# Splitting the second layer's projections into three bf16 parts: the subtractions on TensorE inside the PSUM bank, all casts on ScalarE

## The chip, the cores and the metric

The kernel runs on one core of a Trainium2 chip. A core has five engines, each with its own in-order queue of instructions: TensorE (PE, matmuls), VectorE (DVE), ScalarE (ACT), GpSimd (POOL) and SyncE (SP, which here only issues DMAs). They work on SBUF and on PSUM, whose banks take the matmuls' sums, and they wait for one another through semaphores. The metric is the device time of one execution, in microseconds (us).

## The reference

Four blocks work on x of 4 x 512 tokens x 256, each with a layer norm before it and a residual around it: attention with rotary embedding ("a"), a mixture of experts ("f"), differential attention ("b"), and the mixture of experts again ("h"). The change touches the third:

```python
q = (query @ Wq.T).reshape(B, T, 2 * H, D).transpose(0, 2, 1, 3)   # H = 16, D = 8: 32 heads of 8
k = (query @ Wk.T).reshape(B, S, 2 * H, D).transpose(0, 2, 1, 3)
v = (query @ Wv.T).reshape(B, S, H, 2 * D).transpose(0, 2, 1, 3)
attn = jnp.einsum('bhtd,bhsd->bhts', q * scaling, k)
attn = jax.nn.softmax(attn + causal, axis=-1)
attn = attn.reshape(B, H, 2, T, S)
attn = attn[:, :, 0] - lam * attn[:, :, 1]     # lam = exp(sum(lq1 * lk1)) - exp(sum(lq2 * lk2)) + const
```

## The kernel before

Scores are computed with bf16 operands and yet near fp32's precision: each value of q and k is written as the sum of three bf16 parts, high, middle and low (high is the cast of the value, middle the cast of what is left, low the cast of what is then left). The 8 numbers of a head times 6 products of parts fill 48 rows of a matmul.

**The prologue of layer "b"** makes these parts. It goes over B = 4 batches of 512 tokens, each in eight pieces k = 0 to 7, and every engine has its own function that lists its share of the pieces in a fixed order: `pe_piece`, `dve_piece_b`, `act_proj_b`, `pool_attn`, `sp_attn`. For one batch:

- k = 0 to 2: TensorE turns the normed tiles (`pe_turn`, L1295), ScalarE copies them out (`act_tile_T`, L612).
- k = 1 to 3: TensorE computes v (`pe_v`, L1315) in the two banks `pair_ps[:, 0, 0]` and `pair_ps[:, 0, 1]`, ScalarE copies it out (`act_v`, L621 and L622).
- k = 4 to 7: TensorE computes one block of q or k for each piece (`pe_block`, L1354, four fp32 matmul instructions of 512 columns on the same two banks, block i in bank i % 2). Blocks 0 and 2 are q, 1 and 3 are k.
- Split of a block: ScalarE casts the bank to `parts[:, i, 0]` (`act_block`, L641); VectorE subtracts it from the bank into SBUF, `px[:, i]` (`dve_rest`, L836), which frees the bank (`b_rest`); GpSimd casts `px` to `parts[:, i, 1]` and subtracts once more into `parts[:, i, 2]` (`pool_parts`, L492 and L493), which signals `b_lo`.
- SyncE stores the parts of a block to DRAM when `b_lo` comes (`sp_store_parts`, L339 and L342), and once batch 0 is stored begins to load them back as stacks of 48 rows (`sp_stacks`, L319 and L328).
- VectorE also adds up the residual of the next batch (`dve_back`, L1059) and norms it (L813).

**The first score units** are spread over the same pieces. To find the row maxima for the softmax, TensorE computes scores (`pe_first_scores`, L1451 to L1475) and VectorE reduces each pair of banks with a maximum (`dve_first_max`, L956). There are 30 units before the attention proper: 6 in batch 1 (two each after pieces 5, 6 and 7), 12 in batch 2, 12 in batch 3, by `spread = (0, 2, 3, 5, 6, 8, 9, 10, 12)` over the pieces. They alternate between two pairs of banks, so unit i waits until the maximum of unit i - 2 is taken.

**The end of the prologue**: after its last cast ScalarE computes two exponentials for lam (L691), for which it loads a table; VectorE, in piece 7 of the last batch, waits for them (`dve_lambda`, L891) before it takes the maxima of units 28 and 29. Then slots begin: TensorE's first unit of transposed scores (L1426) goes into the pair of banks that the projections used, and so waits for `b_rest` of all 16 blocks; the next score unit waits for the maximum of unit 28. In the slots ScalarE takes exponentials (L706), GpSimd masks (L519), TensorE multiplies by v (L1501), and VectorE goes on with maxima of later slots.

Of the kernel before, what the change touches and what calls it, by code (L numbers as in the profile page):

```python
# [81 lines left out]
def build(nc, ins, out):  # L82
    ctx = ExitStack()
    with ctx:
# [135 lines left out]
        lane_slot = {"f": c_f[:, o + 2:o + 3], "h": c_f[:, o + 3:o + 4]}  # L220
        ident_b = c_b[:, 0:128]
        mask_h = c_b[:, 384:640]
        upper = c_b[:, 640:768]
# [261 lines left out]

        def pool_parts(pool, b, i):


            j = BLOCKS["b"] * b + i
            ch = Chain(pool, sm("parts_chain"), j)  # L490
            pool.wait_ge(sm("b_rest"), j + 1)
            ch(pool.tensor_copy(parts[:, i, 1], px[:, i]))  # L492
            pool.tensor_tensor(parts[:, i, 2], px[:, i], parts[:, i, 1], ALU.subtract).then_inc(sm("b_lo"), 1)  # L493

        def pool_m_split(pool, s, hp):
# [37 lines left out]
        def pool_attn(pool, s):  # L533
            pool.memset(arena2[:, 16 * T // 2:], ONES2).then_inc(sm("k_ones"), 1)
            for b in range(B):
                if s == "a":
                    pool_rotated(pool, b)
                    if b == B - 1:
                        pool_m_split(pool, s, 0)
                    continue  # L540
                if b == B - 1:
                    pool_m_split(pool, s, 0)
                for i in range(BLOCKS[s]):
                    pool_parts(pool, b, i)
            for n in range(SLOT_N):
                for u in range(UNITS):
                    if u == 2 and n % 4 == 2 and n < LAST_S + 1:
                        pool_m_split(pool, s, (n + 5) // 4)
                    pool_causal(pool, s, n, u)
                if s == "b" and n > 0:  # L550
                    pool_combine(pool, n - 1)
            if s == "b":
                pool_combine(pool, SLOT_N - 1)
# [80 lines left out]

        def act_block(act, b, i):

            j = BLOCKS["b"] * b + i
            act.wait_ge(sm("b_pj"), j + 1)
            if b > 0:
                act.wait_ge(sm(f"kept{i}"), kept("b", i, b))  # L640
            act.activation(parts[:, i, 0], pair_ps[:, 0, i % 2], ACT.Copy).then_inc(sm("b_hi"), 1)  # L641

        def act_std(act, k, a, c):
# [32 lines left out]
        def act_proj_b(act):  # L676
            act_std(act, 6, 0, TB)
            for b in range(B):
                act_tile_T(act, "b", b, 0)
                act_tile_T(act, "b", b, 1)  # L680
                for u in range(2):
                    act_v(act, b, u)
# [3 lines left out]
                if b + 1 < B:  # L686
                    act_std(act, 7 + b, TB * (b + 1), TB * (b + 2))
                for i in range(BLOCKS["b"]):
                    act_block(act, b, i)
            act.wait_ge(sm("b_lam"), 1)  # L690
# [138 lines left out]

        def dve_rest(dve, b, i):  # L830

            j = 4 * b + i
            dve.wait_ge(sm("b_hi"), j + 1)
            if b > 0:
                dve.wait_ge(sm("b_lo"), j - 3)
            dve.tensor_tensor(px[:, i], pair_ps[:, 0, i % 2], parts[:, i, 0], ALU.subtract).then_inc(sm("b_rest"), 1)  # L836

        def dve_v(dve, b, u):
# [30 lines left out]
        def dve_piece_b(dve, b, k):  # L869

            if k == 0 and b > 0:
                dve_rest(dve, b - 1, 3)
            if k >= 5:
                dve_rest(dve, b, k - 5)
            if k == 7 and b == B - 1:
# [29 lines left out]
        def dve_prologue(dve, s):  # L905
# [15 lines left out]
            for b in range(B):  # L921
                for k in range(8):
# [8 lines left out]
                    for i in first_units(s, b, k):  # L931
                        dve_first_max(dve, s, i)
            if s == "b":
                dve_rest(dve, B - 1, 3)
            dve.wait_ge(sm(s + "_xnT"), NT)
# [363 lines left out]
        def pe_bank_free(pe, b, i):  # L1299

            pe.wait_ge(sm("b_rest"), BLOCKS["b"] * b + i + 1)

# [43 lines left out]
        def pe_block(pe, b, i):  # L1346
# [6 lines left out]
            for c in range(CE):  # L1353
                mm = pe.matmul(pair_ps[:, 0, i % 2], wqkv[:, c, i * P:(i + 1) * P], xnT2[:, b % 2, c, :],  # L1354
                               start=c == 0, stop=c == CE - 1)
            mm.then_inc(sm("b_pj"), 1)

        def pe_piece(pe, s, b, k):
# [10 lines left out]
            if k == 0:  # L1369
                pe_turn(pe, s, b, 0)  # L1370
                pe_turn(pe, s, b, 1)
            elif k <= 2:
                pe_v(pe, s, b, k - 1)
                pe_turn(pe, s, b, k + 1)
            elif k == 3:
                pe_v(pe, s, b, 2)
                pe_v(pe, s, b, 3)
            else:
                pe_block(pe, b, k - 4)

# [18 lines left out]
        def pe_prologue(pe, s):  # L1399
            for b in range(B):  # L1400
                for k in range(8):
                    pe_piece(pe, s, b, k)
                    for i in first_units(s, b, k):
                        pe_first_scores(pe, s, i)
            for i in rest_units(s):
                pe_first_scores(pe, s, i)
# [99 lines left out]
        def pe_pair_free(pe, s, kind, n, u):  # L1506
# [5 lines left out]
            if i == -RINGP:  # L1512
                pe.wait_ge(sm("a_v_done" if s == "a" else "b_rest"), NT)
            elif i < 0:
# [230 lines left out]
def constants():  # L1745
# [16 lines left out]
    mh = np.concatenate([np.where((64 * half + r % 64)[:, None] > r[None, :], MASK, 0.0) for half in range(2)], 1)  # L1762
    c_b = np.concatenate([np.eye(P), ms, ms, mh, r[:, None] < r[None, :], np.ones((P, P))], 1).astype(np.float32)
    return {"c_f": c_f, "c_b": c_b, "rot": rot.astype(np.float32)}
# [50 lines left out]
```

## Time and profile before

| | |
|---|---|
| time, median of 3 runs | 1389.14 us (1388.66 to 1392.26) |
| the profiled execution, its own time | 1387.43 us |
| its span, first to last instruction | 1385.7 us |
| busy: PE, DVE, POOL, ACT | 1191.4, 889.8, 668.5, 556.5 us |
| mean granted TensorE clock | 0.936 |
| prologue of "b": first turn to first unit of slot 0 | 698.7 to 778.5 us |

Busy time says how much an engine had to do, not whether others waited for it. The prologue of "b" has some 80 of 1386 us, and it must be read for itself: from the order of each engine's instructions in time, with the idle time before each and what ended it.

### The profile page before, as it was taken

How to read it: one execution, taken by the hardware profiler on the slowest of the kernel's cores; microseconds unless marked ns; L12 is line 12 of the kernel's file. 1: busy time of each engine (PE TensorE's matmuls, PEld its weight loads, DVE VectorE, ACT ScalarE, POOL GpSimd, SP SyncE). 2: the span in 40 equal slices, each digit the busy share in tenths (PEclk: the TensorE clock that was granted, in tenths of full speed). 3: DMA queues.
4: the chain of work that ended last, by engine and by line, in shares of the span. 5: the costliest groups of instructions: out<-in, count | busy, mean ns of one | idle time of the engine just before them, and what ended most of it. 6: DMA issues, size and time to landing. Idle time of an engine off the chain costs nothing.

```text
span 1385.7 us, 25635 instructions
## 1 busy us (share of the span) xinstructions
PE 1191.4 (86%) x8822; PEld 699.4 (50%) x8822; DVE 889.8 (64%) x2017; ACT 556.5 (40%) x922; POOL 668.5 (48%) x813
## 2 busy tenths in 40 slices
PE   6888899997899798999577899999868989899990
PEld 2343343432665576777344344444246547577770
DVE  5588888971782354555289799999376625455551
ACT  2125777778221122222132477777922112222220
POOL 4452334344017576666623354555600566766662
PEclk9887999999879999999789999999996989999995
DMA  4424554300904556666555311211080245666657
GB/s 150 130 84 147 194 181 126 103 27 6 347 21 148 149 126 121 102 117 102 90 184 171 117 53 57 59 54 45 2 307 13 90 161 139 114 110 109 112 77 204
DMA packets 137437, 161.10 MB, mean 116 GB/s; under 512 B 17568, under 2 KB 122848, under 8 KB 136800
## 3 DMA queue, kind: packets, MB, share of 16 engines
q1 hardware_dynamic: 107424, 120.09, 27.8%
q0 software_dynamic: 29184, 38.36, 16.3%
q8 instruction: 74, 1.21, 0.4%
q10 hardware_dynamic: 704, 1.02, 0.2%
q14 instruction: 51, 0.42, 0.1%
HBM read 79.54 MB, written 79.08 MB: 114 GB/s over the span
## 4 chain that ended last, share of the span: by engine, by line
PE 51%; DVE 17%; POOL 9%; DMA 8%; issue 7%; ACT 5%; SPq 3%; POOLq 0%; DVEq 0%; ACTq 0%
PE pair_ps L1699 11%; PE o_ps L1501 8%; PE pair_ps L1712 8%; POOL x_slots L559 6%; DVE nm L956 4%; ACT arena L706 4%; DVE bm L956 3%; PE t_ps L1527 2%; PE pair_ps L1451 2%; PE pair_ps L1706 2%; DMA y_h<-xnT,dest 2%; PE pair_ps L1332 2%; PE pair_ps L1431 2%; DMA y_f<-xnT,dest 2%; PE pair_ps L1456 2%
## 5 line engine op out<-in xcount | busy, mean ns | idle before, releaser
L706 ACT ACTIVATE arena<-pair_ps 128x1024 f32<-128x1024 f32 x320 | 323.1, 1025 | 130.9 <-PE pair_ps L1426 75.9
L519 POOL TENSOR_SCALAR_AFFINE_SELECT arena<-arena 128x512 f32<-128x512 f32 (+1 forms) x320 | 174.1, 544 | 250.5 <-ACT arena L706 250.5
L956 DVE TENSOR_REDUCE nm<-pair_ps 128x2 f32<-128x1024 f32 (+1 forms) x192 | 232.8, 1222 | 32.6 <-PE pair_ps L1475 28.7
L1699 PE MATMUL pair_ps<-arena 128*128 x640 | 220.9, 468 | 1.7 <-ACT arena L753 1.7
L559 POOL DMA_INDIRECT x_slots<-y_sb,slot_i x128 | 123.6, 966 | 176.3 <-DVE slot_i L1145 137.9
L1501 PE MATMUL o_ps<-arena 128*9 128x512 f32 (+7 forms) x2048 | 175.8, 438 | 4.0 <-POOL arena L519 4.0
L1712 PE MATMUL pair_ps<-arena 128*128 x640 | 166.9, 383 | 5.8 <-DVE arena L1230 5.8
L571 POOL DMA_INDIRECT y_h<-xnT,dest x80 | 125.2, 1565 | 73.5 <-DVE xnT L1237 30.2
L571 POOL DMA_INDIRECT y_f<-xnT,dest x80 | 125.2, 1565 | 70.9 <-DMA y_f<-xnT,dest 26.6
L956 DVE TENSOR_REDUCE bm<-pair_ps 128x8 f32<-128x1024 f32 x128 | 155.4, 1218 | 4.5 <-PE pair_ps L1475 1.0
L1712 PEld LDWEIGHTS pair_ps<-arena 128*128 128x128 f32 x640 | 121.7, 192 | 52.3 <-issue 14.0
L1225 DVE TENSOR_TENSOR arena<-arena,pair_ps 128x176 f32<-128x176 f32 x160 | 54.1, 338 | 145.1 <-ACT arena L758 144.8
L1699 PEld LDWEIGHTS pair_ps<-arena 128*128 128x128 f32 x640 | 111.0, 194 | 37.5 <-issue 4.5
L758 ACT ACTIVATE arena<-pair_ps 128x176 f32<-128x176 f32 x160 | 50.8, 318 | 179.8 <-PE pair_ps L1699 179.8
L1237 DVE TENSOR_SCALAR xnT<-pair_ps,slot_w 128x256 f32<-128x256 f32 x160 | 77.4, 484 | 41.7 <-PE pair_ps L1712 17.6
L1659 PE MATMUL pair_ps<-arena 128*128 128x512 f32 (+1 forms) x192 | 91.5, 623 | 0.0
L1475 PE MATMUL pair_ps<-c_b 64*128 64x128 bf16 (+1 forms) x1280 | 84.7, 210 | 0.0
L1475 PEld LDWEIGHTS pair_ps<-c_b 64*128 64x128 bf16 x1280 | 60.6, 98 | 33.4 <-issue 4.0
L1451 PE MATMUL pair_ps<-arena 48*128 48x512 bf16 x256 | 51.1, 394 | 22.6 <-ACT arena L706 17.0
L1230 DVE COPY arena<-pair_ps 128x256 f32<-128x256 f32 x160 | 67.8, 424 | 1.8 <-PE pair_ps L1706 1.4
L1706 PE MATMUL pair_ps<-c_f,arena 128*128 128x128 f32 x320 | 61.9, 275 | 6.5 <-DVE arena L1225 6.4
L1426 PE MATMUL pair_ps<-arena 51*128 51x512 bf16 x256 | 50.7, 392 | 18.4 <-DVE bm L956 7.5
(210 smaller groups left out, 1718.1 us busy)
## 6 DMA issues: line engine op xcount, KB each, us to landing
arena<-x_slots SPq DMA_DIRECT2D x160, 132.5 KB, 2.6
arena<-in_w SPq DMA_DIRECT2D x4, 2816.0 KB, 17.3
x_slots<-hw SPq DMA_DIRECT2D x20, 530.0 KB, 3.4
arena<-in_w SPq DMA_DIRECT2D x4, 2048.0 KB, 17.7
arena<-q_a SPq DMA_DIRECT2D x64, 96.0 KB
arena<-q_b SPq DMA_DIRECT2D x64, 96.0 KB
q_a<-arena SPq DMA_DIRECT2D x8, 384.0 KB, 2.7
y_f<-hw SPq DMA_DIRECT2D x6, 512.0 KB, 4.3
```

Source lines behind the costliest of these rows:

```text
L519: pool.affine_select(p, p, pattern, ALU.is_ge, 0.0, base=0, channel_multiplier=-1)\
L559: pool.indirect_dma_start(x_slots, bass.IndirectOffsetOnAxis(ap=slot_i[:, t, k:k + 1], axis=0), y_sb[:, t, :], None).then_inc(sm("scat0" i ...
L571: pool.indirect_dma_start(y_acc[f][j % ACCS], bass.IndirectOffsetOnAxis(ap=dest[:, j:j + 1], axis=0), yt[:, j % XR, :], None, compute_op=A ...
L706: act.activation(p_ring[:, U % RING, :], pair_ps[:, pair_at("T", n, u)].rearrange("p a c -> p (a c)"), ACT.Exp, scale=SCALE).then_inc(sm(" ...
L956: dve.tensor_reduce(dst, src, X, ALU.max, negate=not 2 <= u < 4).then_inc(sm("t_max_done"), 1)
L1451: pe.matmul(ps, q_of(g, h, KQ, 3 * P, T), k_of(s, g, h, KQ, 0, T), start=True, stop=False, skip_group_check=True)
L1475: mm = pe.matmul(blocks[:, :, 64 * half:64 * half + 64], mask_h[lo:lo + 64, half * P:half * P + P], ident_b[lo:lo + 64, lo:lo + 64].unsque ...
L1501: mm = pe.matmul(o_ps[32 * h:32 * h + vw, T - c:T], v_all[:, g, TB * b + j, v0:v0 + vw], p_ring[:, U % RING, a:a + c], start=j == 0, stop= ...
L1659: mm = pe.matmul(st_ps[0:m, k % 2, 512 * a:512 * a + 512], ws13[:, a, e, r:r + m], xnT_all[:, e, b * T:(b + 1) * T], start=e == 0, stop=e ...
L1699: mm = pe.matmul(s_ps[:, q % 2, 0:2 * INTER], xgT[:, q % 2, c, :], w13[:, c, ds(e, 1), :].rearrange("p a i -> p (a i)"), start=c == 0, sto ...
L1706: mm = pe.transpose(st_ps[:, q % 2, c * P:(c + 1) * P], hs[:, q % 2, c * P:(c + 1) * P], ident_f)
L1712: mm = pe.matmul(st_ps[:, q % 2, 512:512 + E], hsT[:, q % 2, c, :], w2[:, c, ds(e, 1), :].rearrange("p a d -> p (a d)"), start=c == 0, sto ...
```

## The change

For layer "b", VectorE's and GpSimd's shares of the split are gone. After ScalarE has cast the high part out of the bank, TensorE adds minus the high part to the bank (a matmul of the bf16 part with minus the identity, accumulating), ScalarE casts the middle part out of the bank, TensorE takes it off in the same way, and ScalarE casts the low part. The bank is free when the low part is cast (`b_lo`), not after one subtraction. The pieces are put together in pairs: blocks 0 and 1 in piece 4; their first subtraction in 5; their second and then blocks 2 and 3 in 6; the first subtraction of those in 7; their second after the first turns of the next batch.

```diff
+        minus_b = c_b[:, 128:256]
...
-        def pool_parts(pool, b, i):
...
-            ch(pool.tensor_copy(parts[:, i, 1], px[:, i]))
-            pool.tensor_tensor(parts[:, i, 2], px[:, i], parts[:, i, 1], ALU.subtract).then_inc(sm("b_lo"), 1)
...
+        def act_middle_b(act, b, i):
+            j = BLOCKS["b"] * b + i
+            act.wait_ge(sm("b_less_hi"), j + 1)
+            act.activation(parts[:, i, 1], pair_ps[:, 0, i % 2], ACT.Copy).then_inc(sm("b_mid"), 1)
+
+        def act_low_b(act, b, i):
+            j = BLOCKS["b"] * b + i
+            act.wait_ge(sm("b_less_mid"), j + 1)
+            act.activation(parts[:, i, 2], pair_ps[:, 0, i % 2], ACT.Copy).then_inc(sm("b_lo"), 1)
...
                 act_tile_T(act, "b", b, 0)
                 act_tile_T(act, "b", b, 1)
+                if b > 0:
+                    act_low_b(act, b - 1, 2)
+                    act_low_b(act, b - 1, 3)
...
-                for i in range(BLOCKS["b"]):
-                    act_block(act, b, i)
+                for i in range(0, BLOCKS["b"], 2):
+                    act_high_b(act, b, i)
+                    act_high_b(act, b, i + 1)
+                    act_middle_b(act, b, i)
+                    act_middle_b(act, b, i + 1)
+                    if i == 0:
+                        act_low_b(act, b, 0)
+                        act_low_b(act, b, 1)
+            act_low_b(act, B - 1, 2)
+            act_low_b(act, B - 1, 3)
             act.wait_ge(sm("b_lam"), 1)
...
-        def dve_rest(dve, b, i):
...
-            dve.tensor_tensor(px[:, i], pair_ps[:, 0, i % 2], parts[:, i, 0], ALU.subtract).then_inc(sm("b_rest"), 1)
...
         def pe_bank_free(pe, b, i):
 
-            pe.wait_ge(sm("b_rest"), BLOCKS["b"] * b + i + 1)
+            pe.wait_ge(sm("b_lo"), BLOCKS["b"] * b + i + 1)
...
+        def pe_less_high(pe, b, i):
+
+
+            pe.wait_ge(sm("b_hi"), BLOCKS["b"] * b + i + 1)
+            pe.matmul(pair_ps[:, 0, i % 2], minus_b, parts[:, i, 0], start=False, stop=False, skip_group_check=True)\
+                .then_inc(sm("b_less_hi"), 1)
+
+        def pe_less_middle(pe, b, i):
+            pe.wait_ge(sm("b_mid"), BLOCKS["b"] * b + i + 1)
+            pe.matmul(pair_ps[:, 0, i % 2], minus_b, parts[:, i, 1], start=False, stop=True, skip_group_check=True)\
+                .then_inc(sm("b_less_mid"), 1)
...
             if k == 0:
                 pe_turn(pe, s, b, 0)
                 pe_turn(pe, s, b, 1)
+                if b > 0:
+                    pe_less_middle(pe, b - 1, 2)
+                    pe_less_middle(pe, b - 1, 3)
...
+            elif k == 4:
+                pe_block(pe, b, 0)
+                pe_block(pe, b, 1)
+            elif k == 5:
+                pe_less_high(pe, b, 0)
+                pe_less_high(pe, b, 1)
+            elif k == 6:
+                pe_less_middle(pe, b, 0)
+                pe_less_middle(pe, b, 1)
+                pe_block(pe, b, 2)
+                pe_block(pe, b, 3)
             else:
-                pe_block(pe, b, k - 4)
+                pe_less_high(pe, b, 2)
+                pe_less_high(pe, b, 3)
...
             if i == -RINGP:
-                pe.wait_ge(sm("a_v_done" if s == "a" else "b_rest"), NT)
+                pe.wait_ge(sm("a_v_done" if s == "a" else "b_lo"), NT)
```

The constants get minus the identity in a place that nothing read, and after the last batch TensorE takes the middle parts of blocks 2 and 3 off before slot 0.

## Rows read from the trace of the kernel before

**Rows 1.** Busy time by stretch: length, five engines (instructions), TensorE's granted clock, DMA share, GB/s

```profile
706.00:724.00 18.00, 15.86 (x61) 8.42 (x60) 13.95 (x37) 6.69 (x19) 9.06 (x10) 1.00 0.54 172
724.00:742.00 18.00, 14.57 (x109) 8.06 (x109) 17.42 (x28) 4.43 (x16) 5.29 (x6) 1.00 0.60 190
742.00:760.00 18.00, 13.36 (x102) 6.90 (x100) 16.55 (x26) 4.47 (x12) 8.09 (x12) 1.00 0.44 142
760.00:782.00 22.00, 16.48 (x116) 7.97 (x112) 16.47 (x21) 7.11 (x13) 7.85 (x10) 0.90 0.50 159
```

**Rows 2.** Groups by line and shape, 700 to 782 us: busy us, mean ns | idle before, releasers

```profile
L1354 PE MATMUL pair_ps<-xnT,wqkv 128*128 128x512 f32 x64 | 30.7, 610 | 1.0 <-DVE arena L836 0.9
...
L956 DVE TENSOR_REDUCE nm<-pair_ps 128x2 f32<-128x1024 f32 x14 | 16.9, 1222 | 3.2 <-PE pair_ps L1475 3.1
...
L836 DVE TENSOR_TENSOR arena<-pair_ps,arena 128x512 f32<-128x512 f32 x16 | 10.9, 681 | 2.0 <-ACT arena L641 2.0
...
L641 ACT ACTIVATE arena<-pair_ps 128x512 bf16<-128x512 f32 x16 | 9.6, 597 | 29.3 <-PE pair_ps L1354 29.2
...
L1059 DVE TENSOR_TENSOR x_sb<-x_sb,arena 128x256 f32<-128x256 f32 x12 | 6.5, 545 | 0.0
...
L1451 PE MATMUL pair_ps<-arena 48*128 48x512 bf16 x28 | 5.8, 417 | 3.3 <-DMA arena<-k_b 1.4 <-DVE bm L956 1.1 <-DVE nm L956 0.6
```

**Rows 3.** Instructions in time, batches 0 and 1: start, us, engine, what, count, idle before

```profile
705.10 3.60 PE L1354 MATMUL pair_ps<-xnT,wqkv 128*128 128x512 f32 x8
...
708.74 0.60 ACT L641 ACTIVATE arena<-pair_ps 128x512 bf16<-128x512 f32 x1 [1.12 <-PE pair_ps L1354]
...
708.91 3.70 PE L1354 MATMUL pair_ps<-xnT,wqkv 128*128 128x512 f32 x8 [0.21 <-DVE arena L836]
...
713.58 1.13 PE L1315 MATMUL pair_ps<-wqkv,xnT 128*128 128x256 f32 x4 [0.53 <-ACT xnT L612]
...
717.58 3.60 PE L1354 MATMUL pair_ps<-xnT,wqkv 128*128 128x512 f32 x8
...
722.57 0.39 PE L1451 MATMUL pair_ps<-arena 48*128 48x512 bf16 x2 [1.40 <-DMA arena<-k_b]
...
723.07 2.36 DVE L956 TENSOR_REDUCE nm<-pair_ps 128x2 f32<-128x1024 f32 x2 [1.10 <-PE pair_ps L1475]
```

**Rows 4.** Instructions in time, batches 2 and 3, TensorE and VectorE

```profile
744.80 0.34 PE L1456 MATMUL pair_ps<-arena 48*128 48x384 bf16 x2 [2.41 <-DVE nm L956]
...
750.71 1.23 DVE L956 TENSOR_REDUCE nm<-pair_ps 128x2 f32<-128x1024 f32 x1 [0.73 <-PE pair_ps L1475]
...
755.85 1.13 PE L1315 MATMUL pair_ps<-wqkv,xnT 128*128 128x256 f32 x4
```

**Rows 5.** Instructions in time, the end of the prologue and the first units of slot 0

```profile
770.49 1.98 PE L1354 MATMUL pair_ps<-xnT,wqkv 128*128 128x512 f32 x4
...
772.51 0.60 ACT L641 ACTIVATE arena<-pair_ps 128x512 bf16<-128x512 f32 x1 [1.75 <-PE pair_ps L1354]
...
773.12 1.28 ACT L691 ACT_TABLE_LOAD   x1
...
774.65 0.16 DVE L891 TENSOR_TENSOR lam<-lam 128x1 f32<-128x1 f32 x1 [2.23 <-ACT lam L691]
...
775.44 1.22 DVE L956 TENSOR_REDUCE bm<-pair_ps 128x8 f32<-128x1024 f32 x1
...
778.54 0.61 PE L1426 MATMUL pair_ps<-arena 51*128 51x512 bf16 x2 [5.30 <-DVE arena L836]
...
779.73 1.23 DVE L956 TENSOR_REDUCE nm<-pair_ps 128x2 f32<-128x1024 f32 x1 [0.74 <-PE pair_ps L1475]
```

**Rows 6.** Busy time by stretch of 2 us, as rows 1, around the start of slot 0

```profile
776.00:778.00 2.00, 0.00 (x0) 0.00 (x0) 2.00 (x3) 0.00 (x0) 0.00 (x0) 0.89 1.04 346
778.00:780.00 2.00, 1.46 (x10) 0.67 (x10) 1.16 (x3) 0.81 (x1) 1.46 (x2) 0.50 0.10 24
```

**Rows 7.** One line's instructions, 640 to 830 us: duration ns minimum/median/maximum, starts, shapes

```profile
L1059 DVE TENSOR_TENSOR x_sb<-x_sb,arena x16: 391/416/1390, 692.6 to 740.3; 128x256 f32<-128x256 f32 x16
```

More of the change, by code:

```diff
@@ L484, in pool_rotated @@
             low(2)
-        def pool_parts(pool, b, i):
-            j = BLOCKS["b"] * b + i
-            ch = Chain(pool, sm("parts_chain"), j)
-            pool.wait_ge(sm("b_rest"), j + 1)
-            ch(pool.tensor_copy(parts[:, i, 1], px[:, i]))
-            pool.tensor_tensor(parts[:, i, 2], px[:, i], parts[:, i, 1], ALU.subtract).then_inc(sm("b_lo"), 1)
         def pool_m_split(pool, s, hp):
@@ L537, in pool_attn @@
                     pool_rotated(pool, b)
-                    if b == B - 1:
-                        pool_m_split(pool, s, 0)
-                    continue
                 if b == B - 1:
                     pool_m_split(pool, s, 0)
-                for i in range(BLOCKS[s]):
-                    pool_parts(pool, b, i)
             for n in range(SLOT_N):
@@ L633, in act_middle, with act_high_b @@
             act.activation(parts[:, i, 1], pswap[:, i], ACT.Copy).then_inc(sm("a_mid"), 1)
-        def act_block(act, b, i):
+        def act_high_b(act, b, i):
             j = BLOCKS["b"] * b + i
@@ L828, in dve_rope @@
                 .then_inc(sm("a_t2"), 1)
-        def dve_rest(dve, b, i):
[L832 to L835, printed above, removed]
-            dve.tensor_tensor(px[:, i], pair_ps[:, 0, i % 2], parts[:, i, 0], ALU.subtract).then_inc(sm("b_rest"), 1)
         def dve_v(dve, b, u):
@@ L869, in dve_piece_b @@
         def dve_piece_b(dve, b, k):
[L871 to L874, printed above, removed]
             if k == 7 and b == B - 1:
@@ L932, in dve_prologue @@
                         dve_first_max(dve, s, i)
-            if s == "b":
-                dve_rest(dve, B - 1, 3)
             dve.wait_ge(sm(s + "_xnT"), NT)
@@ L1354, in pe_block @@
                 mm = pe.matmul(pair_ps[:, 0, i % 2], wqkv[:, c, i * P:(i + 1) * P], xnT2[:, b % 2, c, :],
-                               start=c == 0, stop=c == CE - 1)
+                               start=c == 0, stop=False, skip_group_check=True)
             mm.then_inc(sm("b_pj"), 1)
+        def pe_less_high(pe, b, i):
[6 more added lines that the diff above has]
+                .then_inc(sm("b_less_mid"), 1)
         def pe_piece(pe, s, b, k):
@@ L1404, in pe_prologue @@
                         pe_first_scores(pe, s, i)
+            if s == "b":
+                pe_less_middle(pe, B - 1, 2)
+                pe_less_middle(pe, B - 1, 3)
             for i in rest_units(s):
@@ L1762, in constants @@
     mh = np.concatenate([np.where((64 * half + r % 64)[:, None] > r[None, :], MASK, 0.0) for half in range(2)], 1)
-    c_b = np.concatenate([np.eye(P), ms, ms, mh, r[:, None] < r[None, :], np.ones((P, P))], 1).astype(np.float32)
+    c_b = np.concatenate([np.eye(P), -np.eye(P), ms, mh, r[:, None] < r[None, :], np.ones((P, P))], 1).astype(np.float32)
     return {"c_f": c_f, "c_b": c_b, "rot": rot.astype(np.float32)}
```

## The prediction

> **What bounds the kernel now.** The page's busy shares average four layers, so I read the prologue of "b" by itself, in this order. First the stretches [rows 1]: from 724 to 760 us VectorE is busy for 33.97 of 36 us and TensorE for 27.9, so VectorE is near its limit in batches 2 and 3; from 706 to 724 us it is the other way round, TensorE 15.86 of 18 and VectorE 13.95. ScalarE never passes 40%. Then the groups [rows 2] for the durations. Then the instructions in time, for what ends each wait: TensorE waits 0.21 us for a subtraction and 1.40 us for the first stack from DRAM [rows 3]; later up to 2.41 us for a maximum [rows 4]; and 5.30 us before slot 0, behind a chain that goes through ScalarE's table load, lam, two maxima and the last subtraction [rows 5]. The reader is to see that no engine bounds the 80 us alone: TensorE's order does so in batches 0 and 1, VectorE's maxima do in 2 and 3.
>
> **The durations.** A block's four matmuls take 1.71 us of TensorE's issue: the second block's bank is ready at 708.74, 3.64 us after the first began at 705.10, of which some 0.2 is the run out of the last matmul [rows 3]. A cast out of PSUM is 0.597 us [rows 2], and a hand-over between engines costs about 0.04 (between the table load's end, 774.40, and VectorE's start, 774.65, lie an exponential of about 0.2 and one hand-over [rows 5]). A maximum is 1.22, and 1.13 to 1.14 from start to start when two follow (two take 2.36) [rows 2, 3].
>
> The new matmul, 128 rows, bf16, 512 columns, is not in the trace. From below: two matmuls of 48 rows and 512 columns take 0.39 us together [rows 3] and about 0.42 each [rows 2], running side by side, so one is at least some 0.11 of issue. From above: an fp32 matmul of the same columns, 0.610 from start to end [rows 2] and 0.43 of issue (1.71 / 4). I take 0.22 of issue and 0.40 until its bank can be read, near the bf16 row. One step of a split (subtract, cast) is then 0.04 + 0.40 + 0.04 + 0.60 = 1.08 us. At the upper bound the 32 new matmuls have 32 x 0.21 = 6.7 us more issue, about half of it beside waits; at the lower 3.5 less, of which likewise half counts: +3.4 and -1.8 on the sum.
>
> **What goes.** 16 subtractions of 0.681 (0.60 in a queue) leave VectorE, 9.6 to 10.9 us [rows 2]; 32 instructions leave GpSimd, which only b_lo waits for. What comes: 32 matmuls, 7.0 us of TensorE, and 32 casts, 19.2 us of ScalarE. ScalarE had 22.7 us busy in the 76 of rows 1, so it stays below 60% and costs through its place in the chain. The bank is free after three casts and two subtractions instead of one of each.
>
> **Batch 0.** Blocks 0 and 1 go from 705.10 to 708.5 as before. High 1 is cast 708.74 to 709.34, taken off by 709.8, middle 1 cast until 710.4; low 0 follows on ScalarE at about 710.3 and ends at 710.9, so block 2 begins at 711.0 instead of 708.91 [rows 3]: +2.1. Behind that wait stand blocks 2 and 3 and the next turns. Blocks 2 and 3 end at 714.4; high 3 is 714.6 to 715.2, its subtraction until 715.6, and the turns of batch 1 stand behind it on TensorE, until 715.9; ScalarE casts middle 2 and 3 until 716.3, copies two turned tiles until 716.8, and casts low 2 until 717.3. Only then may v of batch 1 use the bank: 717.3 for 713.58 [rows 3], +3.8. From v to block 0 nothing changes (4.0 us), so block 0 starts at 721.4. The first stack is later by less: low 3 comes at 717.8, its store and the loads issue 1.3 later than before, so it lands at about 723.8. TensorE gets to unit 0 at 725.9 (before 722.57), and the DMA wait of 1.40 is gone; the first maximum starts at 726.4 for 723.07, +3.3.
>
> **Batch 1.** Pieces 5, 6 and 7 used to alternate one block of 1.7 us with two units, so that VectorE always had one. Now units 0 and 1 are followed by four subtraction and cast steps, then two blocks back to back (3.4 us); units 2 and 3 start at 731.1 and 731.5, units 4 and 5 at 732.9 and 734.0, each held by the maximum two before. The sixth maximum ends at 736.2, 9.8 us after the first began, where six in a row would take 6.9. **Batch 2.** VectorE has 12 maxima (13.6), the residual and norm of batch 3 as before, and no subtractions any more (-2.4). It is fed until the maximum of unit 14 at 752.1 to 753.2; TensorE meanwhile does low-part waits and blocks 2 and 3 (752.6 to 756.0), unit 15 comes at 756.0, and its maximum starts at 756.5 for 750.71 [rows 4], after 3.3 us of idling. So what the missing subtractions give is spent again, and v of batch 3 starts at 760.45 for 755.85 [rows 4]: +4.6. **Batch 3.** v ends at 766.05, blocks 0 and 1 are 766.4 to 769.8, block 2 waits for low 0 until 773.1, block 3 runs 774.8 to 776.5; before, it ran 770.49 to 772.2 [rows 5]: +4.3.
>
> **The end.** Low 2 and low 3 are now cast ahead of lam: high 3 until 777.35, its subtraction, middle 3 until 778.4, its subtraction behind units 28 and 29 until 779.4, low 3 until 780.3. Then table load 1.28 and exponential 0.22 to 781.8, lambda 0.79 on VectorE (774.65 to 775.44 [rows 5]), the maximum of unit 28 at 782.6 to 783.8, that of 29 until 784.95, the memset of the bank 0.48. Slot 0's first unit starts at 780.35, which helps nobody, since the score unit behind it waits for the maximum of 28. The first maximum of slot 0 starts at 785.4 for 779.73 [rows 5]: +5.7. From there VectorE's queue sets the pace of the slots with the same work, and nothing later changes.
>
> One thing may come back. TensorE's granted clock fell to 0.50, that is 1.2 GHz, at the end of its 5.30 us wait, and stayed there for the first units [rows 6]; it held 1.00 through the waits of up to 2.41 us [rows 1, 4]. Now it pauses from 779.4 to 783.9, with 0.3 us of work at 780.35. If the clock holds, a pair of score matmuls takes 0.39 [rows 3] and not 0.61 [rows 5], and five such pieces on slot 0's way win about 1 us. I count half of the chance, -0.5. Sum: 5.7 - 0.5 = +5.2 us. The profiled execution, 1387.4, becomes 1392.6; it lies 1.7 below the median of the runs, 1389.1, so the median becomes 1394.3.
>
> The residual sum of VectorE took 0.545 on average in this stretch [rows 2] where its median is 0.416 [rows 7], 12 x 0.13 = 1.6 us in all, and the longest 1.39. The Trainium skill (SBUF — State Buffer, "SBUF: two separate sides") says that a VectorE instruction with two SBUF inputs and a GpSimd instruction lock each other out of a shared port pair; by it the GpSimd work that leaves would give VectorE these 1.6 us back, and the sum would be +3.6 if VectorE were bound there. I keep +5.2: the long ones can only lie in batches 0 and 1, where TensorE's order sets the pace.
>
> **Rivals.** *VectorE is the bound all along* (the side of not slower). Place: the stretch from the first maximum, 723.07, to that of slot 0, 779.73 [rows 3, 5]. There 11 of the 16 subtractions lie (those of batches 2 and 3, three of batch 1), 6.6 us at 0.60. If TensorE feeds VectorE as well as now, the 3.3 us lost before come back and 3.3 more: 1385.8. It decides whether VectorE's idle time in that stretch grows: at +3.3 us the two cancel, my walk has it grow by about 9. For it speaks [rows 1]; against, that units 1 to 2 and 14 to 15 now lie behind two blocks and a split. *Only batches 0 and 1 lose*: later stalls overlap with VectorE's slack, and of +5.2 some 1.5 is left, 1390.6. *The clock falls in the prologue too*: TensorE now stops for 0.5 to 1 us at four to six places in each batch. At 1.2 GHz a batch's blocks, v and subtractions, 6.8 + 3.0 + 1.8 us, take 11.6 more, of which about 5 beyond waits: +10, 1399. Against it: 1.00 with waits of up to 2.41 [rows 1, 4]. The Trainium skill (TensorE: Matmul & The Clock Gate, "A second HAM failure mode: psum-queue depth-cycling") tells of such an oscillation in a kernel that goes from bank to bank with small pauses; by that rule this rival would be the case.
>
> **How the numbers follow.** About 0.3% (4.2 us) is what a measurement of this kernel can tell from no change. Forecast, own range +2 to +8.5 (the bounds of the matmul, -1.8 and +3.4, about the sum): 0.57. VectorE bound: 0.16. Only the first batches: 0.16. Clock: 0.11. Slower by over 0.3% holds the clock case and 0.48 of the forecast, 0.59; faster, under 1385.0, a little over half of the VectorE case, 0.09; within, 0.32. The range reaches from 1385.5, which takes in part of the VectorE case, to 1399.5.
>
> **What would show it.** In the profile after: block 2 of batch 0 about 5.9 us after block 0 (now 3.8); v of batch 1 held by a cast of ScalarE, not by a copy of a tile; the first unit without a wait on DMA; VectorE idle some 3 us before the maxima of units 2, 15 and 27 (in batches 1, 2, 3); table load after the last low cast; 59.0 us from the maximum of unit 0 to slot 0's first, where it was 56.66 [rows 3, 5] (58 if the clock stays at 1.00), and no other stage changed. I am wrong if VectorE's idle time grows by less than 3.3 us, if the step of 1.08 is far off, or if ScalarE's casts wait for something that I did not see.

## The result and the profile after

The changed kernel takes 1398.62 us (median of 20 runs, 1390.38 to 1402.13) where the kernel before takes 1390.69 (20 runs): a ratio of 1.005 with a 95% interval of 1.0035 to 1.0065, that is 4.9 to 9.0 us more. A second comparison on another chip, further down, gives 1.0035 (1.0021 to 1.0049). On the first chip it is slower by more than the 0.3% that the prediction named; on the second the interval reaches down to 0.21%.

The two profiled spans, 1385.7 and 1398.3 us, differ by 12.6. Of that 7.5 us lie in the stretch that the change touches, from the prologue's first turn to slot 0's first maximum: 698.69 to 779.73 before, 702.21 to 790.74 after. The other 5.1 lie where the code is the same; in the second pair of profiles (the controls below) the same parts differ by -2.0 us. So I go by the stretch from here on. It is 81.04 us before and 88.53 after, and the controls repeat it within 0.3.

The stretches that answer to [rows 1]: length, busy time of PE, PE's weight loads, VectorE, ScalarE and GpSimd with their instructions, granted clock, DMA share, GB/s.

```profile
709.00:727.00 18.00, 15.66 (x52) 8.12 (x53) 6.78 (x27) 10.13 (x28) 0.00 (x0) 1.00 0.44 143
727.00:745.00 18.00, 15.03 (x108) 7.54 (x107) 12.82 (x20) 8.67 (x20) 0.00 (x0) 1.00 0.60 187
745.00:763.00 18.00, 14.63 (x87) 7.02 (x89) 13.95 (x25) 6.82 (x16) 0.00 (x0) 1.00 0.35 109
763.00:781.00 18.00, 17.16 (x112) 9.35 (x112) 12.66 (x14) 7.95 (x21) 1.08 (x4) 1.00 0.43 134
```

VectorE, which was busy for 17.42 and 16.55 of 18 us in batches 2 and 3, is now busy for 12.66 to 13.95. What it gave up turned into idle time. The groups that answer to [rows 2]:

```profile
L1348 PE MATMUL pair_ps<-xnT,wqkv 128*128 128x512 f32 x64 | 29.4, 602 | 1.2 <-ACT arena L638 1.1
...
L950 DVE TENSOR_REDUCE nm<-pair_ps 128x2 f32<-128x1024 f32 x13 | 15.5, 1214 | 5.5 <-PE pair_ps L1499 5.4
L950 DVE TENSOR_REDUCE bm<-pair_ps 128x8 f32<-128x1024 f32 x12 | 14.3, 1217 | 6.8 <-PE pair_ps L1499 6.7
...
L628 ACT ACTIVATE arena<-pair_ps 128x512 bf16<-128x512 f32 x16 | 9.6, 597 | 19.6 <-PE pair_ps L1348 19.6
L633 ACT ACTIVATE arena<-pair_ps 128x512 bf16<-128x512 f32 x16 | 9.0, 594 | 3.0 <-remote 2.2 <-PE pair_ps L1356 0.7
L638 ACT ACTIVATE arena<-pair_ps 128x512 bf16<-128x512 f32 x16 | 8.8, 602 | 1.8 <-PE pair_ps L1361 1.4 <-remote 0.4
```

The casts cost what they cost before (0.597), and the maxima now wait for TensorE's scores. The instructions in time, which answer to [rows 3]:

```profile
708.99 3.60 PE L1348 MATMUL pair_ps<-xnT,wqkv 128*128 128x512 f32 x8
...
713.27 0.39 PE L1356 MATMUL pair_ps<-arena,c_b 128*128 128x512 bf16 x1 [0.69 <-ACT arena L628]
...
714.35 0.39 PE L1361 MATMUL pair_ps<-arena,c_b 128*128 128x512 bf16 x1 [0.20 <-ACT arena L633]
714.84 3.70 PE L1348 MATMUL pair_ps<-xnT,wqkv 128*128 128x512 f32 x8
...
721.44 1.10 PE L1309 MATMUL pair_ps<-wqkv,xnT 128*128 128x256 f32 x4 [0.74 <-ACT arena L638]
...
730.02 0.39 PE L1475 MATMUL pair_ps<-arena 48*128 48x512 bf16 x2
```

The rows are those of L1356 and L1361, TensorE's first and second subtraction, and of L1348, the blocks. Block 2 starts 5.85 us after block 0 (3.81 before), v of batch 1 is released by a low cast (L638), and the first score unit waits for no DMA. Later (of [rows 4]), TensorE and VectorE:

```profile
756.88 3.70 PE L1348 MATMUL pair_ps<-xnT,wqkv 128*128 128x512 f32 x8 [0.47 <-ACT arena L638]
...
760.51 0.39 PE L1475 MATMUL pair_ps<-arena 48*128 48x512 bf16 x2
...
764.99 1.13 PE L1309 MATMUL pair_ps<-wqkv,xnT 128*128 128x256 f32 x4
```
```profile
756.35 1.22 DVE L950 TENSOR_REDUCE nm<-pair_ps 128x4 f32<-128x1024 f32 x1
761.00 2.36 DVE L950 TENSOR_REDUCE nm<-pair_ps 128x2 f32<-128x1024 f32 x2 [3.43 <-PE pair_ps L1499]
```

VectorE finishes the maximum of unit 14 and idles 3.43 us, until TensorE is through blocks 2 and 3 and comes to unit 15. The end (of [rows 5]), engine by engine:

```profile
778.14 3.70 PE L1348 MATMUL pair_ps<-xnT,wqkv 128*128 128x512 f32 x8 [0.20 <-ACT arena L638]
...
785.69 0.39 PE L1450 MATMUL pair_ps<-arena 51*128 51x512 bf16 x2 [1.05 <-ACT arena L638]
789.26 0.61 PE L1475 MATMUL pair_ps<-arena 48*128 48x512 bf16 x2 [3.17 <-DVE bm L950]
```
```profile
784.46 1.08 ACT L638 ACTIVATE arena<-pair_ps 128x512 bf16<-128x512 f32 x2 [0.74 <-PE pair_ps L1361]
785.57 1.28 ACT L699 ACT_TABLE_LOAD   x1
```
```profile
787.10 0.16 DVE L887 TENSOR_TENSOR lam<-lam 128x1 f32<-128x1 f32 x1 [3.55 <-ACT lam L699]
...
790.74 2.29 DVE L950 TENSOR_REDUCE nm<-pair_ps 128x2 f32<-128x1024 f32 x2
```

The low casts, the table load, lam (VectorE idle 3.55 us for it) and the maxima of units 28 and 29 stand in a row; slot 0's first unit is early and helps nobody, since the score unit behind it waits 3.17 us. The granted clock over this wait, as in [rows 6]:

```profile
786.00:788.00 2.00, 0.09 (x2) 0.00 (x0) 0.73 (x5) 1.97 (x3) 0.00 (x0) 1.00 1.02 336
788.00:790.00 2.00, 0.72 (x6) 0.34 (x6) 2.00 (x2) 0.00 (x0) 0.41 (x1) 0.66 0.74 250
790.00:792.00 2.00, 1.18 (x10) 0.48 (x12) 1.90 (x4) 1.02 (x1) 0.00 (x0) 0.50 0.00 0
```

### The profile page after: what moved, and what is told of

Its sections match the earlier page's. It is cut to its first block, busy times and chain, and to the rows that moved or that the text cites. A ratio compares the mean times of both kernels' runs of the same rounds, so it can differ in the third digit from the quotient of the medians.

```text
span 1398.3 us, 25667 instructions
## 1 busy us (share of the span) xinstructions
PE 1202.7 (86%) x8850; PEld 704.6 (50%) x8854; DVE 878.3 (63%) x2001; ACT 573.4 (41%) x954; POOL 640.1 (46%) x781
## 4 chain that ended last, share of the span: by engine, by line
PE 53%; DVE 17%; DMA 8%; POOL 8%; issue 6%; ACT 6%; SPq 2%; another core or an unknown queue 0%; POOLq 0%; DVEq 0%; ACTq 0%
PE pair_ps L1723 11%; PE o_ps L1525 8%; PE pair_ps L1736 8%; POOL x_slots L546 6%; DVE nm L950 4%; ACT arena L714 4%; DVE bm L950 3%; PE t_ps L1551 2%; DMA y_f<-xnT,dest 2%; PE pair_ps L1730 2%; PE pair_ps L1475 2%; PE pair_ps L1348 2%; PE pair_ps L1326 2%; PE pair_ps L1455 2%; DMA y_h<-xnT,dest 2%
## 5 line engine op out<-in xcount | busy, mean ns | idle before, releaser
L1525 PEld LDWEIGHTS o_ps<-arena 128*9 128x9 f32 (+1 forms) x2048 | 38.8, 93 | 52.1 <-issue 30.3
```

Of the source, the lines that this page charges most:

```text
L1525: mm = pe.matmul(o_ps[32 * h:32 * h + vw, T - c:T], v_all[:, g, TB * b + j, v0:v0 + vw], p_ring[:, U % RING, a:a + c], start=j == 0, stop= ...
```

## The experiments

They ran on three other chips than the first profiles, where the kernel before takes 1467 to 1471 us: e3 to e6 on one, the controls, e1 and e2 on a second, e7 to e9 and the second run of e2 on a third. The kernel before was traced again only on the second; there its stretch is the same within 0.3 us and the added time lies outside it. Times are compared with runs of the kernel before on the same chip; e3, e4, e5, e7 and e9 have one execution each, so only their traces are read, and every line of the table is one trace. It gives the start of the first turn and, counted from it, the starts of block 0, of the first maximum, of the first turns of batches 2 and 3, and of slot 0's first maximum (the stretch). TensorE's first 3.6 to 5.9 us after that turn run at 1.2 GHz (granted 0.50), for a time that differs from trace to trace. So block 0 comes after 6.34 to 7.45 us, by the same code, and the later columns of a line are shifted with it, by up to 1.1 us.

| kernel | first turn | block 0 | first maximum | batch 2 | batch 3 | stretch |
|---|---|---|---|---|---|---|
| before | 698.69 | 6.41 | 24.38 | 30.12 | 54.54 | 81.04 |
| after | 702.21 | 6.78 | 28.30 | 36.61 | 60.51 | 88.53 |
| before, control | 739.49 | 6.34 | 24.08 | 29.83 | 54.24 | 80.74 |
| after, control | 739.66 | 6.52 | 28.05 | 36.36 | 60.27 | 88.29 |
| e3, units between blocks | 742.25 | 7.44 | 28.96 | 36.60 | 62.78 | 91.97 |
| e4, pairs alone | 739.76 | 6.78 | 24.59 | 32.95 | 59.90 | 88.87 |
| e5, low part by VectorE | 740.76 | 6.64 | 27.84 | 34.44 | 59.76 | 89.42 |
| e6, new in batches 2 and 3 | 739.01 | 7.45 | 25.14 | 30.89 | 56.00 | 84.02 |
| e1, after, lam late | 742.20 | 7.20 | 28.72 | 37.03 | 60.94 | 84.62 |
| e2, before, lam late (two runs) | 740.30, 740.03 | 6.73, 6.75 | 24.75, 24.40 | 30.49, 30.14 | 54.91, 54.55 | 78.45, 78.08 |
| e7, no second subtraction | 737.94 | 6.96 | 28.48 | 36.29 | 59.40 | 86.46 |
| e8, copy out in 2 and 3 | 738.49 | 6.53 | 24.25 | 29.99 | 55.02 | 77.69 |
| e9, copy out in all | 739.16 | 6.43 | 27.84 | 33.94 | 58.68 | 81.35 |

**Controls.** The kernel before:

> The kernel before once more, as a control. The first four experiments ran on another chip, where the kernel before takes 1471 us and the traces show granted clocks of 0.90 in the prologue of b, so its own stretch from the first turn to slot 0's first maximum has to be read there. If this call runs on such a chip, I expect 83 to 84 us instead of 81.0; on one like the first, 81.0 within 0.5.

The kernel after:

> The changed kernel once more, as a control: the stretch 88.5 us within 0.5 on a chip like the first and 90 to 91 us on one with the lower clock; the time 0.3 to 0.65% above the kernel before on either.

The granted clock was 1.00 in both from 4 us after the first turn to just before slot 0. In e3 and e6 it was so too, from 5.9 us on, and they ran on the chip of e4; so the falls of the clock inside the prologues of e4 and e5 (below) belong to those kernels or executions and not to a lower clock of the chip throughout. The stretches are 80.74 and 88.29, so the change costs 7.55 us there, and the ratio of the times is 1.0035 (1.0021 to 1.0049), 3.1 to 7.2 us.

**e6: which batches lose.** Batches 2 and 3 are as in the changed kernel, 0 and 1 as in the kernel before; `new(b)` is true from batch 2 on.

```diff
+            elif not new(b):
+                pe_block(pe, b, k - 4)
             elif k == 4:
                 pe_block(pe, b, 0)
                 pe_block(pe, b, 1)
...
```

> A mix: batches 0 and 1 split and ordered as in the kernel before, batches 2 and 3 as in the changed one. By my walk the loss up to the first v of batch 2 (5.9 us in the trace) goes and only what comes later stays: the stretch is 82 to 83.5 us, the time 1 to 2.5 us above the kernel before. If relief of VectorE is worth something where VectorE is busy, it is below 80.5 us and the mix is faster than the kernel before. If the loss lies in batches 2 and 3, it is 86 or more.

The stretch is 84.02, a little above the upper end, but 1.0 us of it is the late block 0 (7.45 for 6.41), which this kernel reaches by unchanged code; without it, it is 83.0, inside the range. From the turn of batch 2 to slot 0's maximum it takes 53.13 us (84.02 - 30.89), the kernel before 50.91, the changed one 51.93. So 6.5 of the control's 7.55 us are lost by the turn of batch 2: 4.0 by the first maximum (28.05 for 24.08) and 2.6 from there on (8.31 for 5.75). Batch 2 itself takes 25.11 us in e6 and 23.91 in the changed kernel, for 24.41; from the turn of batch 3 to slot 0's maximum both take 28.02, for 26.50. Together batches 2 and 3 gain nothing from the relief of VectorE in the form in which this change brings it. The time is 1.0003 times that of before (0.9984 to 1.0022): not to be told from it.

**e4: the pairs by themselves**, with the old split.

```diff
-            else:
+            elif k == 4 or k == 6:
                 pe_block(pe, b, k - 4)
+                pe_block(pe, b, k - 3)
```

> The kernel before, with its own split, but with blocks 0 and 1 both in piece 4 and blocks 2 and 3 both in piece 6. Same stretch (81.0 before, 88.5 after). If the pairing is what costs, 83 to 84 us; if the bank's hold by casts and subtractions is, 80.5 to 81.5.

The stretch is 88.87, far above both. VectorE of this kernel, the first maxima behind a pair in batches 1 and 2:

```profile
769.82 2.36 DVE L956 TENSOR_REDUCE bm<-pair_ps 128x8 f32<-128x1024 f32 x2 [2.52 <-PE pair_ps L1476]
...
797.93 1.23 DVE L956 TENSOR_REDUCE nm<-pair_ps 128x2 f32<-128x1024 f32 x1 [4.06 <-PE pair_ps L1476]
```

So pairs do starve VectorE. In batch 1 this is seen without anything else, at a clock of 1.00: from the first maximum to the turn of batch 2 e4 takes 8.36 us (32.95 - 24.59), the changed kernel 8.31, the kernel before 5.75, and e9 below, with a longer hold and no pairs, 6.10. So pairs by themselves are enough for the 2.6 us that the change loses there. They need not be all of it in the changed kernel: e5 below, with its pairs and a shorter chain, takes 6.60. Behind that turn the clock fell too, three times. Stretches of this kernel:

```profile
771.50:775.00 3.50, 1.60 (x20) 0.89 (x16) 3.50 (x5) 0.66 (x2) 1.76 (x2) 1.00 0.35 118
775.00:778.00 3.00, 2.90 (x14) 2.02 (x14) 2.93 (x7) 0.04 (x1) 1.22 (x2) 0.50 0.79 262
...
802.00:806.00 4.00, 3.92 (x21) 2.54 (x22) 3.26 (x7) 0.81 (x3) 2.35 (x5) 0.57 0.74 245
```

TensorE was busy for 1.60 of 3.50 us, with no wait longer than 0.71 us, and was then granted 0.50. No single wait in this kernel's prologue, from block 0 to the last block, is longer than 1.28 us. This is my third rival, in a variant instead of in the changed kernel. The Trainium skill (TensorE: Matmul & The Clock Gate, "A second HAM failure mode: psum-queue depth-cycling") describes it for short pauses between groups; this trace agrees, as the grant went down to 0.50 and back up three times here. In all it was down for 10.2 us. As an estimate, work that ran at half speed for 10.2 us would take 5.1 us less at full speed, so the clock cost at most 5.1 of the 7.8 us. How the 5.0 us that e4 loses behind the turn of batch 2 (55.92 for 50.91) divide between order and clock is not taken apart.

**e3: the remedy that I derived from it**, units of pieces 4 and 6 between the two blocks.

```diff
...
                 pe_block(pe, b, 2)
+                for i in first_units(s, b, 6):
+                    pe_first_scores(pe, s, i)
                 pe_block(pe, b, 3)
```

> The changed kernel, but TensorE puts the first score units of pieces 4 and 6 between the two blocks of the piece instead of behind both. Measure: the stretch from the prologue's first turn to slot 0's first maximum, 81.0 us before and 88.5 after the change. If pairs of blocks back to back starve VectorE in batches 1 to 3, it falls by 1.5 to 3 us, to 85.5 to 87, and VectorE's waits of about 3 us before the maxima of units 2, 15 and 27 shrink to about 1.5. If only the longer hold of the bank (three casts) costs, it stays at 88 to 89.

Both are wrong: 91.97, 3.4 to 3.7 us longer than the changed kernel (0.7 to 0.9 of it by the late block 0), at a clock of 1.00 until the slots. VectorE's waits of about 3 us did shrink, to 1.35 to 2.15, but there are eight over 1 us now instead of four. Batch 1, from the first maximum to the turn of batch 2, became 0.7 us shorter (7.64 for 8.31), batch 2 became 2.3 longer (26.18 for 23.91) and the rest 1.2 longer (29.19 for 28.02). TensorE in batch 2:

```profile
794.08 0.34 PE L1486 MATMUL pair_ps<-arena 48*128 48x384 bf16 x2 [2.42 <-DVE nm L950]
...
794.52 1.98 PE L1348 MATMUL pair_ps<-xnT,wqkv 128*128 128x512 f32 x4
797.19 0.39 PE L1356 MATMUL pair_ps<-arena,c_b 128*128 128x512 bf16 x1 [0.69 <-ACT arena L628]
...
799.03 1.55 PE L1348 MATMUL pair_ps<-xnT,wqkv 128*128 128x512 f32 x3 [0.37 <-ACT arena L638]
```

Unit 13 waits 2.42 us for a maximum, block 1 stands behind it, and the long split of block 1 begins only then. The kernel before has the same wait [rows 4], with one subtraction behind it; here two subtractions and three casts come behind it. So in batches 2 and 3 taking the pairs apart costs the new split more than it gives. That the late start of block 1's split is the reason is my reading of these rows; no run isolates it.

**e7: the price of a step.** TensorE's second subtraction is left out (the low part is then a second cast of the middle remainder, so the scores are less exact).

```diff
-            act.wait_ge(sm("b_less_mid"), j + 1)
...
         def pe_less_middle(pe, b, i):
-            pe.wait_ge(sm("b_mid"), BLOCKS["b"] * b + i + 1)
-            pe.matmul(pair_ps[:, 0, i % 2], minus_b, parts[:, i, 1], start=False, stop=True, skip_group_check=True)\
-                .then_inc(sm("b_less_mid"), 1)
+            return
```

> The changed kernel with TensorE's 16 subtractions of the middle part left out (so the low part is a second cast of the same remainder and the scores lose precision); all casts, orders and waits for casts stay. Stretch from the first turn to slot 0's first maximum, 88.3 us in the control. I counted 0.40 us and two hand-overs for each such step, exposed twice in each batch while ScalarE's casts stay in a row: 85.5 to 87 us. If a subtraction on TensorE costs nothing but its 0.22 us of issue beside waits, it stays above 87.5. If the casts' place in the chain is all of it, likewise.

86.46, and from the first maximum on 57.98 for 60.24: 1.8 to 2.3 us for 16 steps, which speaks for a price of exposed latency. It is under a third of 16 x 0.48 = 7.7 us, so most are covered. This is one trace, and counted from block 0 it is 2.3 us (79.50 for 81.77).

**e5: a shorter chain at VectorE's cost.**

```diff
+        def dve_low_b(dve, b, i):
+            dve.wait_ge(sm("b_mid"), BLOCKS["b"] * b + i + 1)
+            dve.tensor_tensor(parts[:, i, 2], pair_ps[:, 0, i % 2], parts[:, i, 1], ALU.subtract)\
+                .then_inc(sm("b_lo"), 1)
...
```

> The changed kernel, but the low part is written by VectorE, in one subtraction of the middle part from the bank (16 subtractions of 0.68 us back on VectorE, 16 matmuls and 16 casts fewer). If the number of steps until the bank is free sets the loss, each hold is shorter by 0.4 to 0.7 us and the stretch falls from 88.5 to 86 to 87.5 us. If VectorE is the bound, its 6.6 us of new work between the first maximum and slot 0 lengthen it to 90 or more.

89.42, between the two. The turn of batch 2 comes at 34.44 for 36.36 (-1.9), as by the first theory; from there to slot 0's maximum it is 54.98 for 51.93 (+3.1), as by the second, but with the mean clock at 0.69 to 0.74 between 778 and 784 us, behind that turn. It was at 0.50 for 3.4 us, so by the estimate of e4 the clock cost at most 1.7 of the 3.1.

**e1 and e2: the end.** VectorE's wait for lam moves to slot 1.

```diff
-            if k == 7 and b == B - 1:
-                dve_lambda(dve)
...
                     if u == 2 and n > 0:
+                        if n == 1 and s == "b":
+                            dve_lambda(dve)
                         dve_norm(dve, s, n - 1)
```

> The changed kernel, but VectorE waits for the exponentials of lam only in slot 1, just before it first uses them, and not ahead of the maxima of units 28 and 29. If slot 0 is held by low casts, table load, lam and two maxima in a row, as I counted, the maxima of 28 and 29 come 3.5 to 4 us earlier, TensorE's wait of 3.17 us in slot 0 goes, its clock stays at 1.00, and the stretch falls by 3.5 to 4.5 us against the control. If the order of the pairs of blocks alone sets the loss, the stretch falls by less than 1.

> The same move of lam's wait in the kernel before: there the maxima of 28 and 29 gain 2.5 us, the last subtraction and slot 0 too, so the stretch falls by 2 to 3.5 us against the kernel before. If that holds, about 1.2 us of the changed kernel's loss is the place of the low casts ahead of lam (the difference between the two gains), and this version is 0.1 to 0.3% faster than the kernel before. If VectorE's queue takes it back in slot 0, less than 1 us is left.

From the first maximum to slot 0's: 55.90 for 60.24 (-4.3) in the changed kernel, 53.70 for 56.66 (-3.0) in the one before. So the chain of table load, lam and maxima, in the changed kernel behind the low casts, was the end of both, and 1.3 to 1.4 us of the change's loss is the low casts' place ahead of lam. With lam late, the two kernels take 23.68 and 23.54 us from the turn of batch 3 to slot 0's maximum: the 1.5 us between them there (28.02 for 26.50) are gone but for 0.1. Of the changed kernel with lam late:

```profile
826.11 0.39 PE L1450 MATMUL pair_ps<-arena 51*128 51x512 bf16 x2 [1.05 <-ACT arena L638]
826.33 0.40 PE L1475 MATMUL pair_ps<-arena 48*128 48x512 bf16 x2
```

The wait of 3.17 us between these two is gone. That the clock would then stay at 1.00 was wrong: it was at 0.50 from 829.5 to 832.9 us, behind a wait of 1.45 us. The times, against the kernel before: 1.0021 (1.0000 to 1.0041) and 0.9993 (0.9977 to 1.0009). The second run of e2:

> The kernel before with lam's wait moved to slot 1, once more and with more rounds, beside the version with the copy: the stretch 78.4 us within 0.5, the time 0.1 to 0.25% below the kernel before. If VectorE's queue takes the gain back in the slots, the ratio is 1.000 within 0.001.

78.08 us and 0.9987 (0.9972 to 1.0002): a gain of 3 us in the stretch, which the whole time does not show beyond doubt.

**e8 and e9: a version meant to beat both.** TensorE takes only the high part off, ScalarE copies the remainder to SBUF, GpSimd goes on as before; lam late. FIRST is the first batch treated so, 2 in e8 and 0 in e9.

```diff
+        def act_rest(act, b, i):
...
+            act.wait_ge(sm("b_less_hi"), BLOCKS["b"] * (b - FIRST) + i + 1)
...
+            act.activation(px[:, i], pair_ps[:, 0, i % 2], ACT.Copy).then_inc(sm("b_rest"), 1)
...
                         pe_first_scores(pe, s, i)
+                    if s == "b" and b >= FIRST and k >= 4:
+                        pe_less_high(pe, b, k - 4)
```

> A version meant to beat both, with lam's wait in slot 1. Batches 0 and 1 as in the kernel before; in 2 and 3 TensorE takes only the high part off in the bank, behind the score units of the piece, ScalarE copies the remainder to SBUF, which frees the bank, and GpSimd makes the middle and low parts as before; no pairs. VectorE loses its 8 subtractions there (4.8 us in a queue) and the bank is held for two ScalarE steps and one subtraction. If VectorE's relief counts once the hold is short and the blocks stay apart, the stretch is 75 to 77.5 us (78.4 with only lam moved) and the time 0.2 to 0.45% below the kernel before. If TensorE's extra waits eat it, it is 78.5 or more and nothing is gained over lam alone.

> The same in all four batches. In 0 and 1 VectorE has slack, so its relief is worth nothing there and each block's step on TensorE and ScalarE adds 0.5 to 0.8 us: the stretch is 1.5 to 4 us longer than with batches 2 and 3 alone. If a short hold costs nothing in any batch, it is equal within 1 us.

e8's stretch is 77.69, just outside what I hoped for and 0.4 to 0.8 us below e2's (0.2 to 0.6 counted from block 0). From the turn of batch 2 to slot 0's maximum, the second run of e2 and then e8:

```profile
770.17:818.11 47.94, 37.12 (x273) 19.89 (x268) 42.79 (x63) 12.77 (x36) 17.61 (x24) 1.00 0.54 168
```
```profile
768.48:816.18 47.70, 38.81 (x281) 20.75 (x276) 38.11 (x55) 17.25 (x44) 18.41 (x24) 1.00 0.53 168
```

VectorE is busy for 4.7 us less, and 4.4 of them became idle time. But TensorE is busy for 1.7 us more, so this is the net of the relief and of its price and not the relief by itself. VectorE in batch 2, first of e8, then of e2:

```profile
790.22 1.23 DVE L964 TENSOR_REDUCE nm<-pair_ps 128x2 f32<-128x1024 f32 x1 [1.51 <-PE pair_ps L1492]
793.02 1.23 DVE L964 TENSOR_REDUCE nm<-pair_ps 128x2 f32<-128x1024 f32 x1 [1.57 <-PE pair_ps L1492]
```
```profile
792.06 1.23 DVE L954 TENSOR_REDUCE nm<-pair_ps 128x2 f32<-128x1024 f32 x1 [0.74 <-PE pair_ps L1475]
...
794.35 1.23 DVE L954 TENSOR_REDUCE nm<-pair_ps 128x2 f32<-128x1024 f32 x1 [0.47 <-PE pair_ps L1475]
```

Between the two maxima lie a block and a unit on TensorE, in e8 with the new subtraction and its wait for the cast: 2.80 us from start to start there, 2.29 in e2. A maximum takes 1.2, so VectorE waits in these pieces in both, and what it is spared cannot shorten them. Over all of batch 2 e8 loses 0.6 us (25.03 for 24.42), and from the turn of batch 3 on it gains 0.9 (22.67 for 23.53). e9 loses 3.7 us against e8, as expected for batches 0 and 1. In time e8 is 0.9978 of the kernel before (0.9955 to 1.0000), the lowest measured here, at the edge of what can be told; it isn't shown to be faster than e2.

## Why the prediction came out as it did

The direction and the mechanism were right, and the sum was a quarter to a third too small: +5.2 for about +7.0 us in the time and +7.5 in the stretch. The time itself, 1398.62, is 4.3 above the forecast 1394.3 and just inside the upper end of the range, 1399.5; of the 4.3, 1.6 are the start from a median of 3 runs (1389.14), where 20 runs give 1390.69. The trace puts the 7.55 us so: 4.0 by the first maximum, 2.6 from there to the turn of batch 2, -0.5 in batch 2, 1.5 in batch 3 and at the end. By the prediction's own steps:

- *Durations.* The new matmul is 0.379 to 0.390 us from start to end in the trace after (0.40 taken), and from the end of a cast to the end of the next it is 1.08 (713.22 to 714.30), as predicted. The step was right.
- *Batch 0.* Block 2 5.85 us after block 0 (5.9 predicted); v of batch 1 later by 4.3 (721.44 - 702.21 for 713.58 - 698.69), 3.8 predicted; the first maximum by 3.9, 3.3 predicted. Right, and e6, which leaves the new split out of batches 0 and 1, and e9, which adds a longer hold there, show that this is where most of the loss is made. 0.4 us of both is TensorE's start, since block 0 came 6.78 us after the first turn and not 6.41.
- *Batches 1 to 3.* VectorE's idle times before units 2, 15 and 27 were predicted at about 3 us; measured 3.07, 3.43 and 3.13; a fourth, of 2.84 before unit 24, was not named. From the first maximum to slot 0's it is 60.2 us where 59.0 were predicted. VectorE was not busy for 7.5 of 56.66 us before and 17.7 of 60.23 after, by 10.3 us more; I had said 9, and 3.3 as the point where gain and loss cancel. This is what decided between my forecast and the first rival:

```profile
730.51:790.74 60.23, 48.72 (x333) 24.67 (x334) 42.48 (x60) 26.53 (x61) 1.49 (x5) 0.98 0.50 160
```

- *The term that was mis-sized* is the pair of blocks: "then two blocks back to back (3.4 us)". From a pair's first matmul to the score unit behind it are 3.63 us (756.88 to 760.51), not 3.42. All five pairs with a score unit behind them show 3.63, and 5 x 0.21 = 1.05 us. The lag behind my walk grows with them: v of batch 3, with three such pairs ahead of it, comes 5.6 us later than before and not 4.6, of which 0.4 is the start.
- *The clock.* I counted half of 1 us for the case that it holds in slot 0. It fell to 0.50 there, as before the change: 0.5 us more. These two terms, 1.05 and 0.5, make up most of the 2.3 us between +5.2 and +7.5; the start of batch 0 gives 0.4.
- *The end.* 1.36 us predicted as the extra of the low casts ahead of lam (5.7 against 4.3); e1 and e2 give 1.3 to 1.4. The step was right.
- *Rivals.* "VectorE is the bound all along" fell: its idle time grew by 10.3 us, far over the 3.3. e8 agrees, with single blocks: of 4.7 us taken from VectorE in the stretches where it was busiest, 4.4 became idle time, though part of that is the work that TensorE got for it. "Only batches 0 and 1 lose" is nearly what the traces show within the prologue, yet its further step, that later slack absorbs the loss, fails: of the lag of 6.5 us only 0.5 is made good in batch 2, and the rest is carried to the end. "The clock falls in the prologue" did not happen in the changed kernel and did in e4.
- *The shared port.* The residual sums, [rows 7] before, after the change:

```profile
L1053 DVE TENSOR_TENSOR x_sb<-x_sb,arena x16: 391/393/426, 696.1 to 749.1; 128x256 f32<-128x256 f32 x16
```

The longest is 0.426 us where it was 1.390, with GpSimd's subtractions gone. This agrees with the rule of the Trainium skill (SBUF — State Buffer, "SBUF: two separate sides") that a VectorE instruction with two SBUF inputs and a GpSimd instruction that reads SBUF lock each other out. That it brought nothing, as I had said, is not tested by a run; for it speaks that VectorE's queue stood idle for 9.85 us at one stretch in batch 0 after the change, waiting for ScalarE.

What stays open is how the 3.1 us that e5 loses from batch 2 on, and the 5.0 of e4, divide between the order and the lower clock, and what the relief of VectorE would be worth in batches 2 and 3 without more work on TensorE. Open too is how the 2.6 us of batch 1 divide between the pair and the longer chain: no kernel was run with the new split and single blocks in batch 1 and pairs in 2 and 3.

## What to carry to other kernels

An engine that is busy for 95% of a stage need not be what bounds it: first ask what its next instruction will wait for once there is less for it to do, since in e8 4.7 us taken from VectorE, at a price of 1.7 us on TensorE, shortened the prologue by 0.4 to 0.8. Where a buffer passes between engines, count the steps until it is free and what stands behind the waiting instruction on each in-order engine; here pairs with the short chain starved the consumer behind them in batch 1 (2.6 us in e4), while with the long chain taking them apart made batches 2 and 3 longer (e3), so the order must be chosen again when the chain changes length. A wait that nothing needs yet, such as lam's behind a table load, belongs just before its first use.

## What the runs showed of the hardware

- TensorE's granted clock fell to 0.50 three times inside e4's prologue, where no single wait was above 1.28 us, though it held 1.00 through single waits of 2.41 and 2.42 us in other kernels (before, e3).
- After the same first turn of this prologue the clock came up to 1.00 only 3.6 to 5.9 us later, from trace to trace, which moved block 0 by up to 1.1 us.
- The first score matmul behind a pair of fp32 blocks starts 3.63 us after the pair's first matmul, in all five places, and a 128-row bf16 matmul in the same place after 3.43 to 3.54.
- An accumulating bf16 matmul onto a bank that ScalarE has just read starts 0.05 us after the cast ends and costs 0.38 to 0.39 us; ScalarE's independent casts of 0.6 us queue at about 0.49 from start to start where nothing holds the second (1.08 to 1.09 for two).
- The kernel before takes 1391 us on one chip and 1468 on another, and the 81 us of this prologue are the same on both, within 0.3.
